# Folding the feed-forward weights inside the first chunk and taking the first softmax maxima inside the last one

## The reference

```python
x = x + attn_a(layernorm(x))   # each token sees 44 earlier tokens: offsets 0..40, 96, 128, 384
x = x + ffn(layernorm(x))
x = x + attn_b(layernorm(x))   # full attention with rotary positions, not causal
x = x + ffn(layernorm(x))
```

## Time and profile before

| | |
|---|---|
| median of three runs | 2613.07 us |
| profiled execution, its own time | 2615.01 us |
| its span, first to last instruction | 2613.2 us |
| busy share of the span: PE, DVE, ACT, POOL | 92%, 78%, 56%, 28% |
| instructions in the span | 49018 |
| mean granted PE clock | 0.957 of full speed |

### The profile page before, as it was taken

One profiled execution on the slowest core, in us unless ns is written; L12 is line 12 of the kernel. 1 busy time (PEld: TensorE's weight loads), 2 busy tenths in 40 slices (PEclk: granted clock), 3 DMA queues, 4 the chain that ended last, 5 costly groups with the idle time before them and its releaser, 6 DMA issues. The chain is left out here.

```text
span 2613.2 us, 49018 instructions
## 1 busy us (share of the span) xinstructions
PE 2406.7 (92%) x15112; PEld 939.8 (36%) x15112; DVE 2038.7 (78%) x2445; ACT 1468.8 (56%) x2704; POOL 727.3 (28%) x936
## 2 busy tenths in 40 slices
PE   9688999999997648999999999999999999999678
PEld 7234455455445302323333333333333333333144
DVE  5388999999996348888888888888888888888145
ACT  0133444444434104777777777777777777777610
POOL 0688787787773033002002011020000000000110
PEclk9789999999998757999999999999999999999989
DMA  8334444554455197004004013031000000000161
GB/s 286 97 80 112 117 132 125 142 137 114 121 139 147 56 156 85 6 10 59 4 11 61 3 30 41 3 52 19 4 19 4 10 11 4 11 12 3 44 166 40
DMA packets 244668, 174.70 MB, mean 67 GB/s; under 512 B 105804, under 2 KB 215508, under 8 KB 244564
## 3 DMA queue, kind: packets, MB, share of 16 engines
q1 hardware_dynamic: 213048, 116.06, 16.9%
q0 software_dynamic: 13216, 36.72, 9.4%
q10 hardware_dynamic: 18304, 20.59, 2.7%
HBM read 116.49 MB, written 48.05 MB: 63 GB/s over the span
## 5 line engine op out<-in xcount | busy, mean ns | idle before, releaser
L1167 DVE TENSOR_REDUCE mx<-ps_m 128x1 f32<-128x1024 f32 x1036 | 1219.9, 1219 | 253.2 <-PE ps_m L1043 246.7
L1151 ACT ACTIVATE pr<-ps_s 128x512 f32<-128x512 f32 x2048 | 1114.9, 598 | 409.8 <-PE ps_s L1072 385.4
L1072 PE MATMUL ps_s<-qs,ks 99*128 (+1 forms) x2048 | 702.3, 382 | 9.9 <-ACT pr L1151 4.3
L1043 PE MATMUL ps_m<-ks,qs 96*128 (+1 forms) x2072 | 637.7, 389 | 39.9 <-DMA qs<-q_d 33.5
L1081 PE MATMUL ps_o<-pr,vg 128*32 128x512 f32 x4096 | 545.5, 605 | 0.2
L564 POOL TENSOR_TENSOR prod_p<-qT,kT 128x512 f32<-128x512 f32 x336 | 414.0, 1262 | 106.4 <-PE PSa L607 85.4
L1072 PEld LDWEIGHTS ps_s<-qs,ks 99*128 (+1 forms) x2048 | 195.8, 96 | 641.9 <-issue 441.0
L1000 POOL DMA_DIRECT2D vg<-vb_d x24 | 19.8, 824 | 1166.9 <-PE ps_o L1081 1166.5
L1043 PEld LDWEIGHTS ps_m<-ks,qs 96*128 (+1 forms) x2072 | 198.4, 98 | 252.3 <-issue 44.5
L815 DVE TENSOR_TENSOR prod_d<-PSa,kT 128x512 f32<-128x512 f32 x368 | 232.8, 678 | 25.0 <-PE PSa L607 15.5
L607 PE MATMUL PSa<-prod_p,sj 128*32 128x512 f32 x672 | 202.8, 617 | 10.0 <-DVE prod_d L815 7.5
(11 more groups left out here) (134 smaller groups left out, 2090.4 us busy)
## 6 DMA issues: line engine op xcount, KB each, us to landing
own<-skew SPq DMA_DIRECT2D x64, 512.0 KB
ks<-k_d POOLq DMA_DIRECT2D x42, 256.0 KB, 9.2
qs<-q_d POOLq DMA_DIRECT2D x168, 64.0 KB, 9.4
skew<-attn SPq DMA_DIRECT2D x64, 164.0 KB, 4.2
w<-in_W SPq DMA_DIRECT2D x32, 256.0 KB, 4.7
w<-in_W2T SPq DMA_DIRECT2D x32, 256.0 KB, 6.1
vb_d<-vb SPq DMA_DIRECT2D x8, 1024.0 KB, 5.3
q_d<-qparts ACTq DMA_DIRECT2D x16, 384.0 KB, 2.6
```

Source lines behind the costliest of these rows:

```text
L1043: mm = pe.matmul(ps_m[:, u % 2, kc * CH:(kc + 1) * CH], qs[0:KROWS, bass.ds(nq, 1), j, qt * P:(qt + 1) * P].rearrange("p a t -> p (a t)"), ...
L1072: pe.matmul(ps_s[:, op % SB, :], ks[:, bass.ds(slot, 1), j, kt * P:(kt + 1) * P].rearrange("p a t -> p (a t)"), qs[:, bass.ds(q, 1), j, :] ...
L1151: act.activation(pr[:, kt % 4, j, :], ps_s[:, op % SB, :], ACT.Exp, scale=HD ** -0.5).then_inc(p_ready, 1)
L1167: dve.tensor_reduce(mx[:, j * TILES + qt, half:half + 1], ps_m[:, u % 2, :], AX_X, ALU.max).then_inc(m_read, 1)
```

## The change

Four things are changed together.

1. The fold stage is gone as a block. Its pieces are steps `fold_load`, `fold`, `fold_out` in the hand-written lists of `local_stage`, all in chunk 0: pieces 0 to 11 on PE before slot 0, the others among the slots up to position 24.27. The ring is 4 pieces, PSUM for it is single, and b2 is added by a second matmul on PE. SP issues all 32 loads in its one queue with the skews and other loads. The constants move to ACT's queue.
2. The softmax of the local stage: the mask is added only for the first three tiles of a batch; DVE takes a negated maximum; ACT takes eight exponentials of 128x44, one for each head, with the maximum as bias and the sum as accumulator output; DVE inverts and scales. The gain is folded in `wo` once. PE's next `logits` waits for the exponentials. LEAD is 0.5, and all positions of the lists are new.
3. The maxima of the first iteration of the full attention, and 12 units' worth of the second's, are 44 steps `ahead` of two 128x512 units each in the drain, with loads issued by POOL (`ahead_load`) once all products are done. `full_attention` begins with iteration 1. Memory of `ks` and `qs` is shared with the local stage's buffers.
4. POOL loads the constants of the final stage and the inputs of its first two chunks near the end of the full attention; the other six chunks are loaded in the final stage as before.

```diff
-LEAD = 1.0
+LEAD = 0.5
-def fold_ffn(nc, W1, W2T, b1, b2, mt_d, bc_d):
...
 PE_STEPS = [
-    (-11.78, "h_mean", 0), (-9.43, "h_var", 0), (-8.37, "h_back", 0), (-5.34, "k", 0), (-4.42, "q", 0), (-0.38, "v", 0),
...
+    (-13.53, "fold", 0), (-12.84, "fold", 1), (-12.14, "h_mean", 0), (-10.65, "fold", 2), (-9.84, "h_var", 0),
...
+    (23.45, "fold", 30), (24.08, "logits", 4), (24.11, "pv", 1), (24.27, "fold", 31), (24.67, "turn", 2), (25.02, "edge", 2),
+    (25.7, "logits", 5), (26.49, "fold_out", 7), (26.82, "pv", 2), (27.21, "turn", 3), (27.79, "edge", 3),
+    (28.74, "logits", 6), (29.3, "pv", 3), (29.45, "ahead", 0), (30.59, "turn", 4), (30.62, "ahead", 1), (31.28, "edge", 4),
...
+ONCE = {"fold_load": 0, "fold": 0, "fold_out": 0, "gain": 0, "ahead_load": NG - 1, "ahead": NG - 1, "ahead_rows": NG - 1}
+FOLD_RING = 4
+AHEAD_Q = GRP * TILES * NCH
+AHEAD_MAX = AHEAD_Q + AHEAD_Q * 6 // 16
+AHEAD_RUNS = [range(n, n + 2) for n in range(0, AHEAD_MAX, 2)]
...
@@ sync: fold_load
+                    need(sp, piece_used, i - FOLD_RING + 1)
+                    need(sp, acc_step, FOLD_K * (i - FOLD_RING + 1))
+                    for w, src in enumerate((I["W1"], I["W2T"])):
+                        sp.dma_start(fold_w[:, r, w], src[g, rows, :].rearrange("(k p) n -> p k n", p=P)).then_inc(fold_ld[r], 16)
@@ gpsimd
+            def ahead_load(n):
+                if n == 0:
+                    for s in range(2):
+                        pool.wait_ge(qparts_stored[s], 32 * NCH)
+                    pool.wait_ge(prod_d_used, NG * N_DVE)
+                    pool.wait_ge(prod_p_ready, NG * N_POOL)
+                    pool.wait_ge(fold_stored, 32 * NG)
+                rows = slice(HD * n, HD * (n + 1))
+                pool.dma_start(ks[rows, 0, :, :], D["k_d"][K_STACK[n], :, 0:GRP, CH:CH + T]).then_inc(ahead_ld, 16)
+                for x in range(2):
+                    pool.dma_start(qs[rows, x, :, :], D["q_d"][Q_STACK[n], :, 0:GRP, (1 + x) * CH:(2 + x) * CH]).then_inc(ahead_ld, 16)
@@ tensor
+            def fold(i):
+                g, r = i // PIECES, i % FOLD_RING
+                need(pe, fold_sb, g)
+                pe.wait_ge(fold_ld[r], 32 * (i // FOLD_RING + 1))
...
+            def fold_bias(g):
+                pe.wait_ge(acc_step, (g + 1) * PIECES * FOLD_K)
+                pe.matmul(PS[0:1, TAIL_BANK[0], C:2 * C], column[:, :], acc[:, :], start=True, stop=False)
+                pe.matmul(PS[0:1, TAIL_BANK[0], C:2 * C], ident[0:NG, g:g + 1], b2s[:, :], start=False, stop=True).then_inc(fold_ps, 1)
+            def ahead(u):
+                x, head, tile, kc = ahead_place(u)
+                if u == 0:
+                    pe.wait_ge(ahead_ld, 16 * 18)
...
+                need(pe, ahead_read, u - 2)
+                pe.matmul(PS[:, AHEAD_BANKS[u % 3], :], qs[0:KROWS, x, head, tile * P:(tile + 1) * P],
+                          ks[0:KROWS, 0, head, kc * CH:(kc + 1) * CH], start=True, stop=True).then_inc(ahead_ps, 1)
                 elif what == "logits":
-                    need(pe, masked, w)
+                    need(pe, exp_ready, w)
@@ scalar
-                    act.activation(attn[:, w % 2, :, :], lg[:, :, :], ACT.Exp).then_inc(exp_ready, 1)
+                    for h in range(8):
+                        ex = act.activation(attn[:, w % 2, h, :], logits[:, h, :], ACT.Exp, bias=red[:, w % 2, 0, h:h + 1],
+                                            accum_out=red[:, w % 2, 1, h:h + 1])
+                    ex.then_inc(exp_ready, 1)
@@ vector
+                elif what == "fold":
...
+                            dve.wait_ge(acc_step, n)
+                            dve.scalar_tensor_tensor(out=acc[:, :], in0=fold_w[:, r, 1, k, :], scalar=weight, in1=acc[:, :],
+                                                     op0=ALU.mult, op1=ALU.add).then_inc(acc_step, 1)
+                elif what == "fold_out":
+                    dve.wait_ge(fold_ps, i + 1)
+                    dve.tensor_copy(mt[:, :, :], PS[:, TAIL_BANK[0]:TAIL_BANK[1] + 1, 0:C])
+                    dve.tensor_copy(bc[:, :], PS[0:1, TAIL_BANK[0], C:2 * C]).then_inc(fold_sb, 1)
+                elif what == "ahead":
+                    for u in AHEAD_RUNS[i]:
+                        x, head, tile, kc = ahead_place(u)
+                        dve.wait_ge(ahead_ps, u + 1)
+                        dve.tensor_reduce((mx0, mx1)[x][:, head * TILES + tile, kc:kc + 1], PS[:, AHEAD_BANKS[u % 3], :],
+                                          AX_X, ALU.max).then_inc(ahead_read, 1)
@@ full_attention
-            pe.wait_ge(k0_ld, 16 * 12)
-            for u in range(MAXU):
-                max_unit(u, u, 0, 0)
-            max_rows(0, 0)
-            pe.wait_ge(q0_ld, 16 * (6 * (NCH - 1) + 1))
-            for u in range(CARRY):
-                max_unit(u, MAXU + u, 1, 0)
-            pe.wait_ge(nmt_sb, 1)
+            pe.sem_inc(m_ps, MAXU + CARRY)
+            pe.sem_inc(nmt_ps, 1)
             iteration(1, 0, 0, 0, ((1, 0), (2, 0)), (0, 0), first=True)
+            pool.wait_ge(o_stored, 16 * 8 * HG * NCH)
+            for c in range(EARLY):
+                load_totals(pool, D, F["total"][:, c], c, F["total_ld"][c])
+                load_outputs(pool, D, F["oT"][:, c], c, F["o_ld"][c])
+                load_rest(pool, D, F["xc"][:, c], F["mtc"][:, c], F["bcc"][:, c], c, F["x_ld"][c])
@@ final_stage
+            for c in range(EARLY, NG):
+                load_totals(sp, D, total[c], c, total_ld[c])
+                load_outputs(sp, D, oT[c], c, o_ld[c])
```

More of the change, by code:

```diff
@@ L72 @@
 RANK = [ON_POOL[:_m].count(ON_POOL[_m]) for _m in range(END)]
-def fold_ffn(nc, W1, W2T, b1, b2, mt_d, bc_d):
[L77 to L162, removed]
-                        step = dve.scalar_tensor_tensor(out=acc[:, s, :], in0=w, scalar=b1s[:, g, k:k + 1], in1=acc[:, s, :],
-                                                        op0=ALU.mult, op1=ALU.add)
-                    step.then_inc(acc_step, 1)
-                    if k % KP == KP - 1:
-                        dve.wait_ge(acc_step, g * OC + k + 1)
-                        dve.sem_inc(weighted, 1)
-                dve.sem_inc(acc_ready, 1)
-                if g:
-                    output(g - 1)
-            output(NG - 1)
-        @block.scalar
-        def _(act):
-            for g in range(NG):
-                s = g % 2
-                act.wait_ge(evac, g + 1)
-                act.dma_start(mt_d[g + 1].rearrange("(k p) n -> p k n", p=P), mt[:, s]).then_inc(stored[s], 16)
-                act.dma_start(bc_d[g + 1].unsqueeze(0), bc[:, s]).then_inc(stored[s], 16)
-            for s in range(2):
-                act.wait_ge(stored[s], 32 * (NG // 2))
@@ new lines, in local_stage @@
+        fold_room = qs[:, 0:2, :, :].rearrange("p n j t -> p (n j t)").bitcast(F32)
+        mt = fold_room[:, 0:512].rearrange("p (k n) -> p k n", k=KC)
+        acc = fold_room[:, 512:768]
+        bc = fold_room[0:1, 768:1024]
+        b2s = fold_room[0:NG, 1024:1280]
+        b1s = fold_room[:, 1280:1344].rearrange("p (g k) -> p g k", g=NG)
+        column = fold_room[:, 1344:1345]
+        fold_ld = [sem("fold_ld" + str(n)) for n in range(FOLD_RING)]
+        bias_ld, piece_used, acc_step, fold_ps, fold_sb, fold_stored, late_ld = (
+            sem(n) for n in ("bias_ld", "piece_used", "acc_step", "fold_ps", "fold_sb", "fold_stored", "late_ld"))
@@ L585, in _ @@
                     products(j, i)
+                elif what == "ahead_load":
+                    ahead_load(i)
                 else:
@@ L689, in step @@
                     pe.wait_ge(o_sb, (j + 1) * UNITS)
+                    pe.wait_ge(gained, KC)
+                    pe.wait_ge(fold_sb, NG)
                     need(pe, vb_sb, 2 * j)
@@ L1305, in _ @@
                 pe.wait_ge(x_added, n)
-                ln.mean(pe, BANKS_LN, xc[:, c])
+                ln.mean(pe, BANKS_LN, xc[c])
                 if more:
```

549 lines of the change are left out of this document (352 added, 197 removed).

## The result

| | before | after |
|---|---|---|
| median | 2614.86 us (4 runs) | 2538.92 us (4 runs, 2537.24 to 2542.07) |
| profiled execution, own time; span | 2615.01; 2613.2 us | 2537.85; 2536.1 us |
| mean granted clock | 0.957 | 0.972 |

What follows compares the result with a forecast made beforehand. Four stretches with little in parallel, together 345 us, and PE for the rest, bound the kernel. Span: 2613.2 - 20 (fold) - 7 (softmax) + 13 (drain) - 78 (attention's start) - 17 (final stage) = 2504.2; median 2504, range 2460 to 2560.

Steps and rivals of the forecast that it cites:

- the drain's term: Last product to end of the local stage: 124.8 us becomes 138 with the added maxima, bounds 0 and +30.
- By the lists I count 10 us so: Last tail of the drain: 27 pairs of maxima around layernorms, ffn and qk delay the chain by 10 us.
- I take 12 us for both: Drain: PE's wait at the first `ahead` for 18 loads, plus skews slowed by these loads, cost 12 us.
- I take 9 back: Drain: with more work for PE the clock should dip less, returning 9 us.
- the drain hides nothing: Drain: the added maxima cost +56 us instead of +13, time 2547; chance 0.08.
- First chunk: Local stage's start: fold moved into chunk 0, first product at 46 us, chunk 109 us, gain 20, bounds 0 and 33.
- the 28 us for sums held by POOL: First chunk: 40 fold sums on DVE each take 0.7 us more beside POOL's products, 28 us.
- fold still serial in effect: First chunk: PE idles as before and the fold's 65 us come on top, time 2548; chance 0.02 of its own.
- Softmax in the steady part: Chunks 2 to 8: DVE's savings mostly off the path, ACT's extra covered, gain 7 us; bounds gain 25, loss 30.
- the exponentials hold PE's logits: Steady chunks: a us a unit in 56 units, +56 us for -7, time 2567; chance 0.12.
- Attention's start: Full attention's prologue: 82.5 us go, 4 us of waiting for values remain, gain 78; bounds 1 and 12 on the wait.
- Final stage: Block start to first mean: 30.8 us becomes 13.6 through early loads, gain 17, bounds 10 and 19.

Runs made afterwards that it cites:

- reordered run: Changed kernel with q loads in chunk 4, k loaded head by head, and tail maxima as single units in six banks at new places; 2498.77 us (0.9549).
- that run: Changed kernel with all 44 `ahead` steps moved behind the last tail step, their 18 loads still issued behind the last product; 2563.72 us (0.9803).
- the old split: Changed kernel, new order kept, with DVE subtracting the maximum and summing and ACT taking one 128x352 exponential; 2545.35 us (0.9725).

## Why the prediction was right or wrong

**The step that failed** is the drain's term: "124.8 + 13 = 138", measured 166.3. Three parts of it:
- "where a gap is shorter than its pairs the chain slips. By the lists I count 10 us so": this was 27 us, 7.9 among the units and 18.8 in the tail. I had DVE's idle sum right (68 us) and did not follow PE: three banks mean that of each run of units all but the first few wait for DVE, 0.6 us a unit, with the tail's next step behind them, and the clock stayed low. The reordered run shows that it is the order with its banks, not DVE's 56 us of work: the same work costs nothing in a tail of 66.5 us.
- "I take 12 us for both: the wait of PE and the slower skews": 12.6 measured, by the slower skews alone, since no `ahead` waited in that run. PE's wait at the first `ahead`, 7.4 us, is not in the 12.6; it ended (805.50) together with ACT's wait for the late store (805.76). With the `ahead` steps in place the loads were worth 17.2 (80.2 against 63.0). So one of the two mechanisms is shown, and the size was near by luck.
- "I take 9 back" for a warmer clock: nothing came back. The drain's halves ran at 0.77 and 0.70 where they had run at 0.88 and 0.73. More work for PE did not raise it while the work came one unit at a time; in the reordered run, with the same work, it rose to 0.89 and 0.91. So the amount of work did not decide; that the waits did is likely, and no run shows it by itself.

Together 26.7 + 12.6 + 2.2 left over = 41.5 for my 13. The rival "the drain hides nothing" (2547) came within 8 us of the time but is not the case: of 52.7 us of serial work the drain still hid half, and the loads took half of that again.

**First chunk.** -20.6 to the last scores copy of the stage from this term, forecast -20, by two errors that cancel. First product at 45.2 (46 forecast). Chunk 0 took 99.7 us and not 109, since PE sets it; the 28 us for sums held by POOL were 10.7, and off the path. Chunk 1 took 3 us more, not 7 less. The experiment with the fold in front gives the term back with 21.7. The small rival "fold still serial in effect" was added up wrongly: 71.6 us out and 65 in leave a gain of 6.6 and not a loss of 24, so about 2518 and not 2548 by its own rows.

**Softmax in the steady part.** Forecast -7, measured 0: 548.8 us for six chunks in both, DVE's busy time down by 100 us and PE's unchanged. That DVE's time was mostly off the path was right. The step that failed is that the new order of steps was put at nothing: with the old split in it the six chunks take 561.4 us, 12.6 more than before the change, and the new split gives about as much back. PE's waits for DVE are gone and its waits for ACT's copies have come, 13.9 us at `edge` where it was 1.5, 9.1 there and 10.0 at `turn` with the old split. The rival "the exponentials hold PE's logits" looked at `logits`; the place was `edge`, and 12.4 us more in 41 units are 0.3 us each, a third of the rival's price.

**Attention's start and end.** -80.2 (82.1 less 1.9 more in the attention) for -78. Final stage: -19.1 up to the first mean, 1.3 given back, -17.8 for -17. Undone by itself it costs 17.3 us by the medians and 21.2 in the profiled execution.

The errors: -0.6 on the fold, 7 on the softmax, 28.5 on the drain, -2.2 on the attention's start, -0.8 on the final stage, together 31.9; forecast span 2504.2, measured 2536.1.

## What to carry to other kernels

When work is put into another stage's idle time, the idle time of the engine that does it is only half the account: follow its producer too, and count how many results it can leave lying before it must wait, because from then on every step queued behind it waits at the consumer's pace. Look at what the fill's own loads push back, here one small store that took 20 us in a crowd, and move what can be loaded earlier or later. When a lighter step and a new order of steps come in one change, price the order too: DVE lost 100 us of busy time and the six chunks stayed as long, while in one and the same order the lighter softmax was worth 2 us a chunk. An in-order engine that is off the path on average can still stand before one short copy on the path.
